# Decay operand, norms, rope tables and the order of seeds and quotients in the mixer's front

## The reference

```
mod = silu(c) @ wmod                     # six vectors per batch: sa, ca, ga, sb, cb, gb
h   = layernorm(x) * (1 + ca) + sa
r, ek, v = sigmoid(h Wr + br), exp(h Wk + bk), h Wv + bv
for t in range(1024):                    # td = exp(b_td), g = exp(global_decay)
    sa_ = ek*v + td*sa_
    sb_ = ek + td*sb_
    wkv = (g*ek*v + sa_) / (g*ek + sb_ + 1e-6)
    mem = 0.3*mem + r*wkv - (mem > 0.05)*0.05
    spk = mem > 0.05
x = x + ga * spk
# then two layers of windowed attention with q*cos*scale + rotate_half(q)*sin*scale (rope), and an MLP;
# then the second block: a linear recurrent unit and a mixture of experts
```

## Time and profile before

| | us |
|---|---|
| median of 3 runs | 556.4 (556.01 to 557.58) |
| the profiled execution | 556.3 |
| its span | 554.5 |
| VectorE busy | 428.7 |
| TensorE busy (matmuls) | 488.6 |
| ScalarE busy | 347.2 |
| GpSimd busy | 341.0 |

### The profile page before, as it was taken

One profiled execution on the slowest core, in us unless ns is written; L12 is line 12 of the kernel. 1 busy time (PEld: TensorE's weight loads), 2 busy tenths in 40 slices (PEclk: granted clock), 3 DMA queues, 4 the chain that ended last, 5 costly groups with the idle time before them and its releaser, 6 DMA issues.

```text
span 554.5 us, 11715 instructions
## 1 busy us (share of the span) xinstructions
PE 488.6 (88%) x4017; PEld 307.7 (55%) x4017; DVE 428.7 (77%) x1171; ACT 347.2 (63%) x1001; POOL 341.0 (62%) x267
## 2 busy tenths in 40 slices
PE   4662047999999999999989999999999999999997
PEld 3232014467777777543457777777544445667775
DVE  6899999889999886556898999985545688466665
ACT  5851004789999997532589999998646526533332
POOL 5685006999999997776899999994010277410000
PEclk9975559999999999999999999999999999999999
DMA  8400002311111112000041111111000000000000
GB/s 289 168 1 1 1 2 83 67 33 41 39 39 32 39 40 87 1 1 0 2 114 41 40 40 36 36 40 40 1 1 1 0 1 1 1 0 20 20 20 20
DMA packets 14880, 19.93 MB, mean 36 GB/s; under 512 B 2362, under 2 KB 8996, under 8 KB 14692
## 3 DMA queue, kind: packets, MB, share of 16 engines
q1 hardware_dynamic: 14532, 19.08, 12.6%
q10 hardware_dynamic: 288, 0.08, 0.1%
HBM read 8.94 MB, written 1.05 MB: 18 GB/s over the span
## 4 chain that ended last, share of the span: by engine, by line
PE 66%; DVE 16%; POOL 8%; ACT 4%; issue 4%; DMA 1%; DVEq 0%; POOLq 0%; ACTq 0%
PE psT L1479 10%; PE psQK L1554 8%; PE psO L1676 6%; PE psO L1608 5%; PE psQK L1883 5%; PE psS L1656 4%; DVE vst L1078 4%; DVE vAB L1082 4%; PE psO L1479 3%; POOL rn L887 3%; PE psS L1955 3%; PE psQK L1690 3%; PE psS L1792 3%; PE psO L1955 2%; PE psQK L1815 2%
## 5 line engine op out<-in xcount | busy, mean ns | idle before, releaser
L561 ACT ACTIVATE prob<-psS,nmx 128x128 f32<-128x128 f32 x256 | 89.9, 377 | 18.2 <-DVE nmx L1218 18.2
L887 POOL TENSOR_TENSOR rn<-ssq,half 128x16 f32<-128x16 f32 x32 | 93.1, 2910 | 6.9 <-DVE ssq L1204 6.8
L879 POOL TENSOR_TENSOR ra<-ra,rb 128x512 f32<-128x512 f32 x64 | 80.5, 1277 | 1.0 <-DVE rb L1186 0.9
L701 POOL TENSOR_TENSOR rst<-mv,half 128x4 f32<-128x4 f32 x24 | 25.7, 1070 | 73.7 <-DVE mv L990 64.0
L1554 PE MATMUL psQK<-wqkv,hsA 128*128 128x512 f32 x128 | 61.2, 596 | 0.9 <-DVE hsA L1167 0.6
L561 ACT ACTIVATION_READ_ACCUMULATOR prob<-psS,nmx 128x1 f32 x256 | 55.6, 217 | 0.0
L1183 DVE TENSOR_TENSOR ra<-psQK,rope 128x512 f32<-128x512 f32 x64 | 43.8, 685 | 9.4 <-PE psQK L1554 9.0
L895 POOL TENSOR_TENSOR qkn<-ra,rn 128x512 f32<-128x512 f32 x32 | 49.5, 1547 | 2.5
L1186 DVE TENSOR_TENSOR rb<-psQK,rope 128x512 f32<-128x512 f32 x64 | 43.5, 679 | 0.0
L682 ACT ACTIVATE gel<-psQK 128x512 f32<-128x512 f32 x32 | 19.1, 597 | 37.5 <-PE psQK L1883 37.5
L1197 DVE TENSOR_REDUCE ssq<-sq 128x8 f32<-128x512 f32 x64 | 41.1, 676 | 1.6 <-ACT sq L501 1.3
(11 more groups left out here) (254 smaller groups left out, 1189.3 us busy)
## 6 DMA issues: line engine op xcount, KB each, us to landing
vAB<-vAB SPq DMA_DIRECT2D x62, 128.0 KB, 2.2
wqkv<-in_wqkv SPq DMA_DIRECT2D x2, 768.0 KB, 7.9
big<-in_x SPq DMA_DIRECT2D x4, 256.0 KB, 4.8
ropeb<-in_rope SPq DMA_DIRECT2D x1, 1024.0 KB, 6.1
big<-in_ew SPq DMA_DIRECT2D x2, 512.0 KB, 4.1
wmod<-in_wmod SPq DMA_DIRECT2D x2, 384.0 KB, 6.2
out<-big SPq DMA_DIRECT2D x3, 256.0 KB, 2.3
w<-in_w SPq DMA_DIRECT2D x2, 341.0 KB
```

Source lines behind the costliest of these rows:

```text
L561: act.activation(prob[:, k, :], psS[:, hb, c * P:(c + 1) * P], ACT.Exp, bias=nmx[:, k:k + 1], accum_out=sums[:, n % 2, k:k + 1]).then_inc( ...
L879: pool.tensor_tensor(o, o, rb[:, r], ALU.add).then_inc(s["sum_" + name], 1)
L887: pool.tensor_tensor(rn[:, :], ssq[:, :], half[:, :], ALU.pow).then_inc(s["rn_ready"], 1)
```

## The change

- The rope table of layer 0 is no longer made by GpSimd. A copy of the table with channels on partitions, `rope_t` (128 x 2 x 1024, 1 MB), is loaded into `ra`; behind `mixer_x` ScalarE scales its two halves by a column of `vec`, TensorE turns them in four groups of four transposes, and ScalarE evacuates the four banks into `rope`. TensorE waits for `rope_ready` ahead of the transposes of the new residual; GpSimd's wait for it is gone.
- The norms of groups 2 and 3 move from ScalarE to GpSimd, as `tensor_scalar` of 128 columns with two column scalars.
- VectorE copies the decay into a column of `psT0`, and the scan L1035 reads it there; L1041 still reads `sc`.
- VectorE's quotients, GpSimd's products of the division and ScalarE's norms and seeds stand in another order.
- TensorE: v(0) comes ahead of t2(1); three and four products of `ident` with itself are put around t2(0), whose results nobody reads; the banks and waits of `receptance` and the wait of `mixer_turn` are others.

```diff
@@ -42,7 +42,8 @@
...
 V_NU, V_TH, V_GAM, V_SGN = 27, 28, 29, 30
-NV = 31
+V_RS = 31
+NV = 33
...
@@ -185,12 +186,12 @@
...
@@ -260,7 +261,13 @@
...
-            return (psQK[:, 0, :], psQK[:, 1, :], psT0[:, :], psS[:, 0, :])[g]
+            return (psQK[:, 0, :], psQK[:, 1, :], psS[:, 0, :], psS[:, 1, :])[g]
+
+        rope_t = ra[:, :].rearrange("p (k t) -> p k t", k=2)
+
+        def rope_bank(n):
+
+            return (psS[:, 0, :], psS[:, 1, :], psQK[:, 0, :], psQK[:, 1, :])[n]
...
@@ -319,6 +326,7 @@
...
             sp.dma_start(wrkv[:, :, :], a["wrkv"]).then_inc(s["ld_wr"], 16)
+            sp.dma_start(rope_t, a["rope_t"]).then_inc(s["ld_rt"], 16)
             sp.dma_start(identb[:, :], a["identb"]).then_inc(s["ld_wa"], 16)
...
@@ -460,26 +468,32 @@
...
             mixer_out(0)
+            mixer_norm(1)
             act.wait_ge(s["kbias"], 1)
...
             act.activation(sc[:, 11:14], fr[:, 12:15], ACT.Exp).then_inc(s["scales"], 1)
-            mixer_norm(1)
             decays(0)
             mixer_out(1)
-            mixer_norm(2)
             decays(1)
+            mixer_out(2)
             seeds(0)
-            mixer_out(2)
-            mixer_norm(3)
             decays(2)
+            mixer_out(3)
             seeds(1)
-            mixer_out(3)
             decays(3)
...
                 mixer_x(g)
+            act.wait_ge(s["ld_rt"], 16)
+            for k in range(2):
+                act.activation(rope_t[:, k, :], rope_t[:, k, :], ACT.Copy, scale=vec[:, V_RS + k:V_RS + k + 1]).then_inc(s["rope_scaled"], 1)
+            for n in range(4):
+                k, h = divmod(n, 2)
+                act.wait_ge(s["rope_turned"], n + 1)
+                act.activation(rope[:, 4 * h:4 * h + 4, 2 * k:2 * k + 2, :],
+                               rope_bank(n).rearrange("p (n c d) -> p n c d", n=4, c=2), ACT.Copy).then_inc(s["rope_ready"], 1)
...
@@ -728,7 +742,18 @@
...
             pool.tensor_tensor(sc[:, 2:3], fr[:, 0:1], vec[:, V_GD:V_GD + 1], ALU.pow).then_inc(s["sc_ready"], 1)
+            def mixer_norm(g):
+
+                n = ln_no(0, g)
+                pool.wait_ge(s["ln_rstd"], n + 1)
+                pool.wait_ge(s["ln_norm"], TPG * n)
+                pool.wait_ge(s["ln_t2"], n - 1)
+                for k in range(TPG):
+                    pool.tensor_scalar(lnx[:, n % 2, k, :], xt[:, g * TPG + k, :], rst[:, n % 4, k:k + 1], nmr[:, n % 4, k:k + 1],
+                                       ALU.mult, ALU.add).then_inc(s["ln_norm"], 1)
+
             ln_rstd(ln_no(0, 2))
+            mixer_norm(2)
             pool.wait_ge(s["scales"], 1)
...
@@ -736,6 +761,7 @@
...
             ln_rstd(ln_no(0, 3))
+            mixer_norm(3)
...
@@ -772,17 +798,17 @@
...
             denominator(0)
+            denominator(1)
             newton(0)
-            denominator(1)
             rough(0)
+            denominator(2)
             newton(1)
-            denominator(2)
             rough(1)
+            denominator(3)
             newton(2)
-            denominator(3)
             rough(2)
+            received(3)
             current(0)
-            received(3)
             current(1)
...
@@ -791,9 +817,6 @@
...
             own.one(pool.tensor_tensor(sc[:, 7:8], fr[:, 0:1], fr[:, 2:3], ALU.pow))
-            pool.wait_ge(s["ld_wa"], 64)
-            rope_tables(0)
-
             C1 = 1.0 / (2 * np.pi)
...
@@ -850,7 +873,6 @@
...
             pool.wait_ge(s["cur_ready"], NG - 1)
-            pool.wait_ge(s["rope_ready"], 4)
             for k, edge in enumerate((hsA[64:128, T:T + 1], hsA[64:128, 0:1], hsM[64:128, T:T + 1], hsM[64:128, 0:1])):
...
@@ -918,6 +940,7 @@
...
                     pool.wait_ge(s["rope_q"], 2 * NT)
+                    pool.wait_ge(s["ld_wa"], 64)
                     rope_tables(1)
...
@@ -1026,11 +1049,13 @@
...
                 ekvp = psO[:, g % 2, :]
-                td = sc[:, 0:1].to_broadcast([P, GW])
+                td = psT0[:, 0:1].to_broadcast([P, GW])
                 last = g * GW - 1
...
                     dve.wait_ge(s["sc_ready"], 2)
+                    dve.tensor_copy(psT0[:, 0:1], sc[:, 0:1]).then_inc(s["td_ready"], 1)
+                    dve.wait_ge(s["td_ready"], 1)
                 dve.wait_ge(s["ek_ready"], g + 1)
...
@@ -1038,7 +1063,7 @@
...
                 dve.wait_ge(s["ekv_ready"], g + 1)
-                own.one(dve.tensor_tensor_scan(sab[:, c], td, ekvp, 0.0 if first else sab[:, last:last + 1],
+                own.one(dve.tensor_tensor_scan(sab[:, c], sc[:, 0:1].to_broadcast([P, GW]), ekvp, 0.0 if first else sab[:, last:last + 1],
                                                ALU.mult, ALU.add))
...
@@ -1053,10 +1078,13 @@
...
-            for g in range(NG):
-                sums_scanned(g)
-                if g:
-                    quotient(g - 1)
+            sums_scanned(0)
+            sums_scanned(1)
+            sums_scanned(2)
+            quotient(0)
+            sums_scanned(3)
+            quotient(1)
+            quotient(2)
             dve.wait_ge(s["den_ready"], NG)
...
@@ -1497,14 +1525,14 @@
...
                 else:
-                    pe.wait_ge(s["r_ready"], 3)
+                    pe.wait_ge(s["num_ready"], NG)
                 four(psT0, lambda k: xt[:, g * TPG + k, :]).then_inc(s["xT_fill"], 1)
...
                     pe.wait_ge(s["mod_fin"], 1)
-                elif g == NG - 1:
-                    pe.wait_ge(s["ek_ready"], NG - 1)
+                elif g >= 2:
+                    pe.wait_ge(s["ek_ready"], g + 1)
                 mm(r_bank(g), wrkv[:, 0, :], hsA[:, gsl(g)], start=True, stop=True).then_inc(s["r_mm"], 1)
...
@@ -1515,23 +1543,37 @@
...
+            def idle_products(times):
+
+                for _ in range(times):
+                    mm(psQK[:, 1, 0:P], ident[:, :], ident[:, :], start=True, stop=True)
+
             modulation(0, psQK[:, 0, :])
+            idle_products(3)
             ln_t2(ln_no(0, 0))
+            idle_products(4)
             pe.wait_ge(s["ld_wr"], 16)
...
                 mm(psS[:, g % 2, :], wrkv[:, 1, :], hsA[:, gsl(g)], start=True, stop=True).then_inc(s["kv_mm"], 1)
-                if g + 1 < NG:
+                if 0 < g < NG - 1:
                     ln_t2(ln_no(0, g + 1))
...
                 mm(psO[:, g % 2, :], wrkv[:, 2, :], hsA[:, gsl(g)], start=True, stop=True).then_inc(s["kv_mm"], 1)
+                if g == 0:
+                    ln_t2(ln_no(0, 1))
             for g in range(NG):
...
                 mixer_turn(g)
+            pe.wait_ge(s["r_ready"], NG)
+            for n in range(4):
+                k, h = divmod(n, 2)
+                pe.wait_ge(s["rope_scaled"], k + 1)
+                four(rope_bank(n), lambda j: rope_t[:, k, (4 * h + j) * P:(4 * h + j + 1) * P]).then_inc(s["rope_turned"], 1)
             pe.wait_ge(s["num_ready"], NG)
...
@@ -1575,6 +1617,7 @@
...
             keep_clock(10, psO[:, 0, :])
+            pe.wait_ge(s["rope_ready"], 4)
             def stack_t1(g):
...
@@ -1985,7 +2028,7 @@
...
         "ident": np.eye(P, dtype=np.float32), "identb": np.eye(P).astype(bf), "masks": masks.astype(bf),
-        "rope": np.ascontiguousarray(rope), "before": np.ascontiguousarray(before),
+        "rope": np.ascontiguousarray(rope), "rope_t": tab.astype(np.float32).reshape(T, 2, P).transpose(2, 1, 0), "before": np.ascontiguousarray(before),
         "tvec": np.arange(T, dtype=np.float32)[None, :],
...
@@ -2009,6 +2052,9 @@
...
     cols.append(np.concatenate([np.ones(64, np.float32), -np.ones(64, np.float32)]))
+    for n in ("q", "k"):
+        v = col(f"L0_ffn_{n}_scale")[0]
+        cols.append(np.concatenate([v, v[DH // 2:], v[:DH // 2]]))
     br, bi, cr, ci = (col("L1_attn_" + n).T for n in ("B_re", "B_im", "C_re", "C_im"))
...
```

More of the change, by code:

```diff
@@ L186, in program @@
         psT1 = ps("psT1", [P, GW])
-        names = """ld_id ld_x0 ld_x1 ld_x2 ld_x3 ld_wm0 ld_wm1 ld_ew ld_c ld_wr ld_wa ld_wq ld_wl ld_lru ld_moe ld_out st_out
+        names = """ld_id ld_x0 ld_x1 ld_x2 ld_x3 ld_wm0 ld_wm1 ld_ew ld_c ld_wr ld_wa ld_wq ld_wl ld_lru ld_rt ld_moe ld_out st_out
             init table edges mod_raw cnt_ready cnt_sum renewed spk hsA_dma1 hsA_dma2 hsA_dma3 silu_c mod_mm mod_fin sc_ready
@@ L192, in program @@
             kv_mm num_ready ek_ready gek_ready ekv_ready sb_ready den_ready r_mm r_ready cur_ready x_mixed
-            kbias halves scales eps_ready seed_ln seed_ready newton_ready rough_ready quot_ready
+            rope_scaled rope_turned td_ready kbias halves scales eps_ready seed_ln seed_ready newton_ready rough_ready quot_ready
             dve dve_b act_own pool_own fallback fallback_b rope_ready tabs_phase tabs_ready z_ready hsA_ready
```

## The result

The changed kernel takes 550.26 us, median of 4 runs (549.83 to 551.66), against 556.5 for the kernel before on the same chip (4 runs, 556.01 to 557.58): a ratio of 0.9898 [0.9886, 0.991]. So 5.7 to 6.2 us are gained where 6.6 were forecast. The time is 0.5 us off the forecast 549.8 and inside the range. The profiled execution took 550.24 us, with a span of 548.4.

A forecast was written before the change was run, and what follows sets the result against it. VectorE's chain up to the spikes, lengthened by waits for and hold-ups beside GpSimd, was taken as the bound. Tables 4.3 plus front 2.3 made 6.6 us off the median 556.4: 549.8, range 548.2 to 552.3.

The forecast's parts named there:

- Tables: Membrane passes: without GpSimd's four rope tables, VectorE's held-up window goes, 4.3 us gained; replacement work hidden, done by 52.
- Front: Stretch before the membrane passes: walking the engines' queues in the new order moves their start from 41.5 to 39.2, gaining 2.3.
- Decay in PSUM: VectorE's scan L1035: no longer held up by GpSimd, 1.22 us in place of 2.29, 1.07 gained at scan 3.
- Norm on GpSimd: Norms of groups 2 and 3 in the front: 1.5 us each on GpSimd, from 0.372 per piece; ScalarE relieved of 3.3.
- Detour of the seeds: Front: eps and its like come 2 us later behind GpSimd's norm; gek(0) waits until 14.75 in place of 14.0.
- rival 1: Front's gain eaten by late seeds if each GpSimd norm costs 2.9 us or more; only tables pay, 552.1; chance 0.17.
- Who ends last: End of the front: GpSimd's current(2) ends last at 38.7, after VectorE's L1063 at 37.4; passes from 38.8.
- Idle products: TensorE around t2(0): passes start at 38.8 if the clock rises before k(0) is through, 40.3 if later; weighed 39.2.
- Last product of the front: VectorE's L1063 at 40.23: 1.21 us beside current(2), of which 0.5 is hold-up and 0.7 its own.
- Rival 3: Membrane passes stall for something other than the tables, or evacuations disturb them; only the front pays, 554.1; chance 0.05.
- rival 4: Slower kernel: GpSimd norms of 5.9 us each move the passes' start to 47.5, 1.7 us beyond the gain; chance 0.04.
- Rival 2: Front gains more: quotients and L1063 meet GpSimd's gaps, passes start at 37, time 547.7; chance 0.12.

The follow-up runs named there:

- e1: Changed kernel with the four rope tables written by GpSimd again, all else kept: 554.99 us, 0.9983 of the kernel before.
- e2: Kernel before with only the rope part of the change (tables by ScalarE and TensorE, 1 MB more loaded): 552.71 us, 0.9933.
- e12: The changed kernel unaltered, timed and profiled a second time beside the kernel before: 549.91 us, 0.9888.
- e3: Changed kernel with the scan of ek reading its decay from SBUF again: 553.83 us, 0.9955 of the kernel before.
- e4: Changed kernel without the seven idle TensorE products: 549.54 us, 0.9887 of the kernel before.
- e8: Changed kernel with GpSimd's small products, norms, denominator 3 and currents and ScalarE's seeds reordered for fewer meetings: median 550.73 us, 0.9903; profiled execution 548.68.
- e9: e8 without the idle products: 549.25 us, 0.988 of the kernel before.
- e7: Changed kernel with the old order of GpSimd's division products and VectorE's quotients: 552.41 us, 0.9935 of the kernel before.
- e10: e8 unchanged, profiled a second time: 550.27 us, span 548.5.
- e6: Changed kernel with GpSimd's three small products (eps first) ahead of its norm of group 2: 549.72 us, 0.989 of the kernel before.
- e5: Changed kernel with the norms of groups 2 and 3 back on ScalarE at their old places: 550.79 us, 0.99 of the kernel before.
- e11: e6 without the idle products: 549.93 us, 0.9894 of the kernel before.

## Why the prediction came out right

**Tables.** The step was exact: 4.3 us from the window of four instructions, 30.5 to 26.2 in e1 and e2, with the old front and the new one. The work that took their place cost nothing in the passes, and ended at 43.96, earlier than the 52 allowed; the scale took 1.09 and not 1.2 to 1.4. No wait of TensorE for rope_ready showed. Only that x, wmod[0] and wrkv come as before is off: the first product of wmod[0] begins 0.2 us later (5.57 for 5.35).

**Front.** Forecast 2.3 (a start of 39.2), measured 1.9 (39.60), and 2.3 in e12 (39.23). The 2.3 counts from the measured start, 41.5, the 2.9 and 1.4 of the branches from the walk's own 41.7, which is 0.2 us of slack in the sum. Step by step:
- *Decay in PSUM.* The mechanism is right and the scan takes 1.21 to 1.28. The price of 1.07 "at scan 3" was that of the old order. In the new one a norm, two scans and a quotient are held up when the decay stays in SBUF, and e3 puts that at 3.8 us. The sum did not suffer, as the walk had the new order with the scans free.
- *Norm on GpSimd.* The term was mis-sized: 1.75 us and not 1.5, since a piece with two column scalars takes 0.44 and the row I took (0.372) has one. With 0.45 a piece the walk had given 39.4; that this is close to 39.60 is no proof, as the next two points show.
- *Detour of the seeds.* As predicted in kind: gek(0) waited (till 15.26, said 14.75), and the gain was not eaten; rival 1 put that point at 2.9 us per norm.
- *Who ends last.* Here the walk was off and the number was not. It had VectorE through with the quotients at 32.9 and with L1063 at 37.4, and the passes held until current(2) ended at 38.7. GpSimd's part came true: current(2) ends at 38.62. But VectorE is 2.1 us behind its walk: quotient 0 comes at 27.07 for 26.1, and the hold-up of quotients 1 and 2 lasts to 35.03 and not to 32.9, since both meet a product. The reciprocal then ends at 38.29, L1091 at 39.53, and that is what the passes wait for. The 39.2 survived because both engines end within a microsecond of each other; that is luck.
- *Idle products.* The prediction left two branches, 38.8 if the level rises before k(0) is through, 40.3 if it rises later, and weighed them. Both came up, and the other way round. The first profile has the early rise (k(0) 1.10) and starts at 39.60: the level falls again at v(1), behind 2.77 us of idle time, and VectorE waits 0.97 and 0.51. The second (e12, k(0) 1.84) and e1 (1.91) have the late rise, with v(1) at the upper level, and start at 39.23 and 39.15. Scan 1 begins at 18.67 to 18.70 in all three, so what k(0) gains is gone by then. Without the products e4 starts at 38.94. So this step was wrong: that the products pay if the rise comes early doesn't hold, the branches are 0.4 us apart and not 1.5, and that their weighed mean, 39.2, lies so near is luck. Removed, the products are no loss on the median.
- *Last product of the front.* I put its 1.20 down to current(2) beside it. No run shows that: it takes 1.18 to 1.21 in the profile of every kernel, always begun 0.3 us before the last current ended, and ends 0.9 behind that end, not 0.55 as the quotients do. No run has it alone, so how much of it is its own is open.

**Behind the passes.** Everything shifted by one amount: 6.15 us at the first transfers behind the spikes (84.02 for 90.17), 6.1 between the spans. **Rivals.** Rival 3 (the tables don't pay) and rival 4 (the norm) are out by e1, e2 and the 1.75. Rival 1's condition (2.9 per norm) was not met. Rival 2's floor of 37 wasn't reached, because both last quotients still meet products; e8's profile, at 37.90, shows how near an order can come. Of the signs of being wrong none showed: norm pieces 0.44 where 0.7 was the bound, waits of 0.97 and 0.51 where it was 1.

**Parts and whole.** Against the changed kernel's medians (549.9 to 550.3) the tables give 4.7 to 5.1 us (e1; 3.9 and 4.2 by the spans, 4.3 in the passes), the decay in PSUM 3.6 to 3.9, the order 2.2 to 2.5, the norms 0.5 to 0.9, which the intervals don't tell from nothing, and the idle products nothing. That is more than the 5.7 to 6.2 of the whole, since the decay's price is so high only in an order that meets the products with its scans: the parts of the front are not to be added.

**Open.** What level each unprofiled execution had; whether e9 is faster than the changed kernel; what the last product would take alone; what decides between a quotient and a product that begin together; where three of e7's runs lose 1.5 us. That e8's four runs spread for the reason that e10 shows is argued from one pair of profiles.

## What to carry to other kernels

List for each stretch which VectorE instructions read two inputs from SBUF and which GpSimd products run beside them; then either put one operand into PSUM (a broadcast column costs one copy of 0.15 us) or take the GpSimd work elsewhere. A few products of 1.25 us beside a chain of short instructions cost nearly their whole length (4.3 of 5.0 us here), and VectorE counts as busy all that time. When queues are re-ordered, walk all of them with durations from rows, and take the small products (eps here) and the form of each instruction (one column scalar or two) seriously: with the durations of the changed kernel such a walk hit the start within 0.4 us in e6, e7 and e8 (0.7 off in e8's second profile), and missed it by 0.7 in e5 and 1.1 in e3; what was expected without a new walk was 0.7 off in e4 and over 2 in e11. What no walk here could know are TensorE's level and who waits when two instructions begin together. And profile one kernel twice before believing a microsecond: here the second profile turned the reading of the idle products round.

## What was not expected of the hardware

- Two executions of one kernel (e8, e10) differed by 1.6 us of span: 0.76 and 0.95 in two places, less 0.1 on the way, both from the level that TensorE had (k(0) 1.12 or 1.85; granted clock 1.00 or 0.64 from 272 to 276 us).
- Work added to raise the level can bring idle time further on, behind which the level falls: k(0) 1.10 and v(1) 1.92 in one profile with it, 1.84 and 1.02 in another, 2.04 and 1.02 without.
- A VectorE quotient and a GpSimd product that begin within 0.01 us of each other: in one profile the product waits (1.82 for 1.27), in four the quotient (1.80 or 1.81 for 0.68).
- One scan with both inputs in SBUF stretches a GpSimd norm beside it from 1.75 to 2.64 us (e3).
- The reciprocal, with one input, takes 3.34 in every kernel with GpSimd products beside it, which run on at 1.25 apiece, where the two-input quotients next to it are held up. No run has it alone.
- A GpSimd piece of 128 columns with two column scalars takes 0.44 us, one with a single column scalar 0.372.
